# Four-layer MetaFormer on one core: units taken in pairs, skip additions moved to VectorE, matmuls added around the attention, and its softmax weights split between PSUM and GpSimd

## Chip, core and metric

The kernel runs on one core of one Trainium2 chip. The metric is device time in microseconds (us) of one launch: the median over repeated runs, lower is better. The rows below come from one profiled execution of the same program.

## What is computed

The reference is a stack of four layers on an image batch of 8 x 64 channels x 16 x 16. Each layer is a convolution-like block followed by a mixture of experts (MoE) over the tokens. The parts that the change touches:

```python
# layers 0 and 2, the MoE: two of eight experts per token, and the token itself is kept (skip)
out = tokens
for e in range(E):
    h = jax.nn.gelu(tokens @ w1[e] + b1[e], approximate=False)
    y = h @ w2[e] + b2[e]
    out = out + combine[:, e:e + 1] * y
# layer 1, the conv block: dilated 3x3 attention, one head pair for each dilation 1, 2, 4, 8
for i, dil in enumerate(DILATIONS):
    attn = jnp.einsum('bhcl,bhcpl->bhlp', qr, ku) * SCALE
    attn = jax.nn.softmax(attn, axis=-1)
    out = jnp.einsum('bhlp,bhcpl->bhlc', attn, vu)
    feats.append(...)
```

A MoE's input is the layer norm of the residual `t`, and its output is added to `t`. So the residual gets `t + ln(t) + experts` in layers 0 and 2.

## The kernel before

**Tiling.** The 2048 tokens lie as 16 tiles of 128 rows (partitions) by 64 channels in `res` (residual) and `xn` (normed). All data stays on the chip. Each engine (PE, DVE, ACT, POOL, SP) has its own instruction list, written out by hand in program order, with semaphores between them. An engine takes its list strictly in order.

**Layer norm and split.** `ln` writes `xn` on DVE. `split` then cuts it in two f16 halves: ACT writes the high half (L377), DVE subtracts it for the low half (`low`, L601, four instructions of 256 columns). PE transposes both (L1180), ACT and DVE copy them to `xs` (L389, L611), and the router's matmuls (L1190) follow.

**A MoE with skip (m = 0 and 2), "turned units".** 16 units (four token chunks of 512 x four expert pairs). For unit k: `first` makes h (L1232, L1233: f16, 512 columns each), ACT takes the gelu (L436), `spread` makes the routing weights over the expert rows (L1241: 16 rows x 512 columns, from `cT`), DVE multiplies (L779) into `gw`, and `turned_second` multiplies by w2 (L1287: f32, two halves of 64 output rows). At the first unit of a chunk, L1282 adds the biases `b2s`. After a chunk ACT copies the sum out (L398), PE turns it back (`turn_back`, L1297), and DVE adds it to the residual (`residual`, L771). The order on PE is `first(k+1)`, `spread(k)`, `turned_second(k-2)`. `spread(k)` needs DVE to be done with unit k-2, since two banks (4 and 5) alternate.

The value `base = res + xn` that L771 adds to is made by GpSimd in one instruction of 1024 columns (`with_skip`, L319), which starts once `xn` is written. In layer 0 GpSimd then also scales and splits the weights of later layers (L294, L305). After the last unit of MoE 0 GpSimd clears the borders ("pads") of the key and value buffer `kvx` (L345, two memsets of 3072 columns).

**The attention of layer 1.** Keys and values are shifted by PE (L1433) and copied by ACT (L508). DVE makes the logit products (L990, 768 columns) for three tap rows r and four dilations i. It reduces those of r = 1 and 2 itself (L997), and PE sums those of r = 0 (L1439, eight f32 matmuls whose moving columns are 8 elements apart). DVE takes the maxima (L1003) and subtracts them (L1009), ACT takes the exponentials (L513) into `le`, in SBUF. DVE multiplies weights by values (L1032, 24 instructions of 384 columns, two for each i and r). PE sums the products of i = 0, 1, 2 (L1444, nine groups of three f32 matmuls), DVE sums the weights (L1041, L1043) and, for i = 3, the products (L1046). `outputs_in` (L1019) divides PE's sums. `keep_warm` (L1196) is a run of matmuls whose result nobody reads.

Of the kernel before, what the change touches and what calls it, by code (L numbers as in the profile page):

```python
# [6 lines left out]
P = 128  # L7
NT = B * H * W // P
HALF = NT // 2
NPIX = H * W  # L10
DILS = (1, 2, 4, 8)
# [61 lines left out]
def metaformer(nc: bass.Bass, dram, codebook, out):  # L73
# [6 lines left out]
    with ctx:  # L80
# [23 lines left out]

        WH, WL = {}, {}
        for _, name in SPLIT + [("", "mix"), ("", "projs")]:
# [90 lines left out]
        cT = sb("cT", [32, NT * P], fp16)  # L197
        b2s = sb("b2s", [16, 2, 64], fp16)
# [4 lines left out]
        HIGH_LAG, LAG, PLAIN_LAG, TURNED_LAG = 2, 5, 3, 2  # L203
# [19 lines left out]
            "h_out act_out cb_out weighted out_added routed b2_both acc_copied acc_T base_ready unit_high unit_low_vec unit_low_pool second_out acc_in "  # L223
            "logit_product logit_summed value_product tap_row_summed kv1_out kv1_in shift_out shift_in att_sub att_exp mix_set mix_out pb_out pbias_in "
# [41 lines left out]
        logit_slots = [slots[4 + n % 4] for n in range(4)] + slots[0:4] + [slots[4 + n % 4] for n in range(4)]  # L266

# [19 lines left out]
        def _(pool):  # L287
# [23 lines left out]
            nc.gpsimd.memset(minus[:, :], -WSCALE / 2).then_inc(S["consts_set"], 1)  # L311
            scale_weights(["wqkv"])
# [3 lines left out]
            def with_skip(m):  # L316

                pool.wait_ge(S["src_ready"], chunks * (SPL.index(f"ln{2 * m + 1}") + 1))
                nc.gpsimd.tensor_tensor(base[:, :, :], res[:, :, :], xn[:, :, :], ALU.add).then_inc(S["base_ready"], 1)  # L319

# [18 lines left out]
            with_skip(0)  # L339
# [19 lines left out]
            with_skip(2)  # L359
# [10 lines left out]
        def _(act):  # L370
# [35 lines left out]
            def moe(m):  # L406
# [23 lines left out]
                if m in SPREAD:  # L430
                    for k in range(N):
# [7 lines left out]
                        if k >= 6 and (k - 6) % units[m] == 0:  # L439
                            copy_out(m, (k - 6) // units[m])  # L440
# [120 lines left out]
        def _(dve):  # L561
# [199 lines left out]
            def turned_units(m):  # L761
                U, N = units[m], chunks * units[m]

                def residual(c):
# [3 lines left out]
                    if c == 0:  # L768
                        dve.wait_ge(S["base_ready"], m // 2 + 1)
# [853 lines left out]
```

## Time and profile before

| what | value |
|---|---|
| median of 3 runs | 502.57 us (501.96 to 503.05) |
| the profiled execution | 502.17 us, its span 500.4 us |
| mean granted TensorE clock | 0.843 of full |
| DVE busy | 422.6 us, 84% of the span |
| PE busy (matmul) | 371.1 us, 74% |
| ACT busy | 210.6 us, 42% |
| POOL busy | 141.9 us, 28% |

The engine that ends a stage changes from stage to stage, so the shares alone decide little: each stage has to be read by itself. The profiled execution's time is 1.8 us more than its span, which is what lies around the span.

### The profile page before, as it was taken

To read this page: it belongs to the slowest core of one execution; us is meant where nothing else is said; L and a number is where in the kernel's file an instruction comes from. 1 tells how busy PE (TensorE), PEld (TensorE's weight loads), DVE (VectorE), ACT (ScalarE), POOL (GpSimd) and SP (SyncE) were. 2 spreads that over 40 slices of the span, in tenths; PEclk is the share of its full clock that TensorE was granted. 3 is DMA by queue.
4 is the path that set the end of the run, shared out by engine and by line. 5 is a ranking of instruction groups with operands and counts; after the bars stand their busy time and mean duration, and the time that the engine had idled before them with its cause. 6 is when DMAs were issued, how large, how long until landed. Compare 5 with 4: busy or idle time off the path is not lost.

```text
span 500.4 us, 9065 instructions
## 1 busy us (share of the span) xinstructions
PE 371.1 (74%) x3258; PEld 194.8 (39%) x3258; DVE 422.6 (84%) x1512; ACT 210.6 (42%) x398; POOL 141.9 (28%) x127
## 2 busy tenths in 40 slices
PE   2848669947797656799997993880369969448996
PEld 1434423314236523356664662260133323114554
DVE  4788987598979988879999999888885497897997
ACT  1642024412401121478885883330034434217994
POOL 1720040040000000078885884011020003711552
PEclk9978779977887858799998997777579987559999
DMA  8700000000000000000000000000000000100000
GB/s 351 298 1 0 1 1 2 0 2 0 0 0 1 0 1 1 0 2 4 1 3 1 2 3 2 0 1 1 0 2 0 1 0 9 27 9 2 12 14 22
DMA packets 2860, 9.73 MB, mean 19 GB/s; under 512 B 512, under 2 KB 1152, under 8 KB 2688
## 3 DMA queue, kind: packets, MB, share of 16 engines
q1 hardware_dynamic: 1296, 5.21, 2.6%
q10 hardware_dynamic: 1008, 3.42, 1.7%
q0 software_dynamic: 512, 0.53, 0.5%
q8 instruction: 26, 0.43, 0.3%
q14 instruction: 18, 0.15, 0.1%
HBM read 8.63 MB, written 0.52 MB: 18 GB/s over the span
## 4 chain that ended last, share of the span: by engine, by line
DVE 32%; PE 17%; issue 7%; ACT 1%; DVEq 0%; ACTq 0%
DVE res L805 13%; PE bank L1232 3%; PE bank L1261 2%; DVE hx L1131 2%; PE bank L1196 2%; PE bank L1233 2%; DVE bst L616 2%; DVE rs L1116 1%; DVE rs L1130 1%; PE bank L1522 1%; PE bank L1520 1%; PE bank L1287 1%; DVE xt L601 1%; DVE kvx_mem L815 1%; DVE xn L632 1%
## 5 line engine op out<-in xcount | busy, mean ns | idle before, releaser
L1196 PE MATMUL bank<-xs 128*128 128x512 f16 x242 | 76.8, 486 | 61.0 <-DVE bst L616 56.0
L326 POOL TENSOR_TENSOR kvx_mem<-kvx_mem 128x512 f16<-128x512 f32 x64 | 74.0, 1159 | 120.7 <-ACT kvx_mem L459 120.7
L805 DVE SCALAR_TENSOR_TENSOR res<-bank,rp,res 128x64 f32<-128x64 f32 x384 | 83.4, 291 | 2.2
L1196 PEld LDWEIGHTS bank<-xs 128*128 128x128 f16 x242 | 28.1, 120 | 105.4 <-DVE bst L616 57.6
L1261 PE MATMUL bank<-w_high,kvx_mem 128*128 128x64 f16 x768 | 58.4, 194 | 2.3 <-POOL kvx_mem L326 1.7
L1261 PE MATMUL bank<-w_low,kvx_mem 128*128 128x64 f16 x768 | 58.1, 194 | 0.0
L1261 PEld LDWEIGHTS bank<-w_high,kvx_mem 128*128 128x128 f16 x768 | 50.8, 98 | 13.8 <-POOL kvx_mem L326 2.0
L1232 PE MATMUL bank<-xs,w_high 128*128 128x512 f16 x128 | 51.5, 402 | 4.6 <-DVE kvx_mem L815 4.6
L377 ACT ACTIVATE xt<-xn 128x256 f16<-128x256 f32 x32 | 11.6, 417 | 101.4 <-DVE xn L634 101.4
L1261 PEld LDWEIGHTS bank<-w_low,kvx_mem 128*128 128x128 f16 x768 | 49.0, 98 | 7.1 <-issue 0.3
L1233 PE MATMUL bank<-xs,w_low 128*128 128x512 f16 x128 | 51.3, 400 | 0.0
L454 ACT ACTIVATE kvx_mem<-bank 128x512 f32<-128x512 f32 x64 | 38.1, 596 | 23.8 <-PE bank L1233 23.8
L815 DVE SCALAR_TENSOR_TENSOR kvx_mem<-kvx_mem,bank 128x512 f32<-128x512 f32 x64 | 44.7, 700 | 3.9 <-ACT kvx_mem L454 3.7
L459 ACT ACTIVATE kvx_mem<-kvx_mem 128x512 f16<-128x512 f32 x64 | 39.6, 622 | 0.0
L426 ACT ACTIVATE kvx_mem<-bank,pack_r 128x512 f32<-128x512 f32 x64 | 37.8, 714 | 0.0
L779 DVE TENSOR_TENSOR kvx_mem<-kvx_mem,bank 128x512 f32<-128x512 f32 x32 | 21.6, 687 | 18.0 <-PE bank L1241 15.7
L363 POOL DMA_INDIRECT kvx_mem<-in_codebook,ix x16 | 15.5, 967 | 56.8 <-DVE ix L1151 53.7
L436 ACT ACTIVATE kvx_mem<-bank,pack_r 128x512 f32<-128x512 f32 x32 | 21.2, 681 | 18.4 <-PE bank L1233 17.5
L336 POOL TENSOR_TENSOR kvx_mem<-kvx_mem 128x512 f16<-128x512 f32 x16 | 18.6, 1163 | 36.0 <-ACT kvx_mem L426 36.0
L1180 PE MATMUL bank<-pack_half,xt 128*128 128x128 f16 x144 | 13.3, 234 | 17.5 <-DVE xt L601 17.3
L1233 PE MATMUL bank<-xs,wu_low 128*128 128x512 f16 x64 | 25.0, 390 | 0.0
L1232 PE MATMUL bank<-xs,wu_high 128*128 128x512 f16 x64 | 25.0, 390 | 0.0
(310 smaller groups left out, 723.9 us busy)
## 6 DMA issues: line engine op xcount, KB each, us to landing
kvx_mem<-in_m SPq DMA_DIRECT2D x1, 2560.0 KB, 13.7
pack_l<-in_l ACTq DMA_DIRECT2D x1, 898.5 KB, 18.6
kvx_mem<-in_m SPq DMA_DIRECT2D x1, 768.0 KB, 18.5
pack_c<-in_c ACTq DMA_DIRECT2D x1, 648.0 KB, 5.7
pack_l<-in_l SPq DMA_DIRECT2D x1, 586.5 KB, 15.4
pack_x<-in_x SPq DMA_DIRECT2D x1, 512.0 KB, 5.5
pack_half<-in_half ACTq DMA_DIRECT2D x1, 512.0 KB, 7.7
pack_c<-in_c ACTq DMA_DIRECT2D x1, 512.0 KB, 14.0
```

Source lines behind the costliest of these rows:

```text
L326: nc.gpsimd.tensor_tensor(gl[:, n % DEPTH, :], gw[:, n % DEPTH, :], gh[:, n % DEPTH, :], ALU.subtract).then_inc(S["unit_low_pool"], 1)
L426: nc.scalar.activation(dst[:, n % DEPTH, :], bank[k % 4][:, :], ACT.Gelu, bias=K["b1_3"][:, k % units[m]:k % units[m] + 1], scale=1 / WSCA ...
L436: nc.scalar.activation(g[:, n % DEPTH, :], bank[k % 4][:, :], ACT.Gelu, bias=K[f"b1_{m}"][:, k % units[m]:k % units[m] + 1], scale=1 / WSC ...
L454: nc.scalar.activation(g[:, n % DEPTH, :], bank[k % 2][:, :], ACT.Silu, scale=1 / WSCALE)\
L459: nc.scalar.activation(gh[:, n % DEPTH, :], gw[:, n % DEPTH, :], ACT.Copy)\
L779: V.tensor_tensor(gw[:, n % DEPTH, :], g[:, n % DEPTH, :], bank[4 + k % 2][:, :], ALU.mult)\
L805: last = V.scalar_tensor_tensor(res[:, x, :], bank[4 + j % 4][:, 64 * t:64 * t + 64], rp[:, x, e:e + 1], res[:, x, :], ALU.mult, ALU.add)
L815: V.scalar_tensor_tensor(gw[:, (n0 + k) % DEPTH, :], g[:, (n0 + k) % DEPTH, :], CSCALE / WSCALE, bank[2 + k % 2][:, :], ALU.mult, ALU.mult ...
L1196: T.matmul(bank[unused][:, :], xs[:, 0:P], xs[:, 0:512], start=True, stop=True)
L1232: T.matmul(dst[:, :], WH[name][:, P * un:P * un + P], x, start=True, stop=False)
L1233: mm = T.matmul(dst[:, :], WL[name][:, P * un:P * un + P], x, start=False, stop=True)
L1261: mm = T.matmul(out_bank[:, 64 * t:64 * t + 64], part[:, n % DEPTH, P * t:P * t + P], w[f"w2_{m}"][:, 64 * un:64 * un + 64], start=(cfg["s ...
```

## The change

It has these parts.

1. **Paired units** (MoE 0 and 2). PE takes two units at a time: `first` of two, `spread` of two, then `turned_second` of the two before. `spread` and the bias matmuls now read 128 rows of `cT`, `sel0` and `b2s` instead of 16; the rows above 16 are cleared by GpSimd at the start.
2. **Skip additions on VectorE.** `with_skip` is gone from GpSimd. DVE adds `xn` into `res` in four instructions of 256 columns for each of the two MoEs, between the units. GpSimd's weight work of layer 0 now waits for `b2_ready`, which DVE signals at the end of the routing.
3. **Pads.** GpSimd clears only the columns that are read (eight memsets of 96 to 768 columns) and does so once the first k/v projection is done.
4. **Warm attention.** `keep_warm(8)` ahead of the shifts, `keep_warm(10)` ahead of the logit sum.
5. **Attention weights.** For dilations 0 to 2 ACT writes the exponentials to PSUM (banks 0 to 2), and PE's sums move to banks 4 to 6. For dilation 3 they stay in SBUF, and GpSimd makes the products (six instructions of 384 columns). DVE sums the weights by additions in place of the reduction, after i = 1, and sums dilation 3's products by four additions in place of L1046.

```diff
-            with_skip(0)
+            pool.wait_ge(S["b2_ready"], 1)
             scale_weights(["convw", "cbT"])
             weight_lows(["convw", "cbT"])
-            pool.wait_ge(S["second_out"], chunks * units[0])
-            for x in (0, PADX + NT):
-                nc.gpsimd.memset(kvx[:, :, x:x + PADX, :, :].rearrange("p r x a c -> p r (x a c)"), 0.0)\
-                    .then_inc(S["pads_set"], 1)
+            pool.wait_ge(S["kv1_out"], 1)
+            for i, d in enumerate(DILS):
+                for x in (PADX - d, PADX + NT):
+                    nc.gpsimd.memset(kvx[:, :, x:x + d, :, 16 * i:16 * i + 16], 0.0).then_inc(S["pads_set"], 1)
+            pool.wait_ge(S["pads_set"], 8)
+            pool.wait_ge(S["att_exp"], 4)
+            for r in range(3):
+                for h in range(2):
+                    value_product(nc.gpsimd, slots[6 + r], le[:, 3, 3 * r:3 * r + 3, :], r, 3, h)\
+                        .then_inc(S["value_product_pool"], 1)
...
-                nc.scalar.activation(le[:, :, 3 * r:3 * r + 3, :], lg[:, :, 3 * r:3 * r + 3, :], ACT.Exp, scale=8 ** -0.5)\
+                nc.scalar.activation(exps(r)[:, 0:3, :, :], lg[:, 0:3, 3 * r:3 * r + 3, :], ACT.Exp, scale=8 ** -0.5)\
                     .then_inc(S["att_exp"], 1)
+            nc.scalar.activation(le[:, 3, :, :], lg[:, 3, :, :], ACT.Exp, scale=8 ** -0.5).then_inc(S["att_exp"], 1)
...
+                def add_skip(c):
+                    t = slice(4 * c, 4 * c + 4)
+                    V.tensor_tensor(res[:, t, :], res[:, t, :], xn[:, t, :], ALU.add).then_inc(S["skip_added"], 1)
...
-                else:
-                    outputs_in(i - 1)
-            seq(V.tensor_reduce(stk[:, :, 48:64], pool_prod[:, :].rearrange("p (t x c) -> p x c t", t=9, c=16), AX,
-                                ALU.add))
+                if i == 2:
+                    outputs_in(0)
+                    outputs_in(1)
+            outputs_in(2)
+            dve.wait_ge(S["value_product_pool"], 6)
+            row3 = pool_prod[:, 0:768]
+            seq(V.tensor_tensor(row3, row3, pool_prod[:, 768:1536], ALU.add))
+            seq(V.tensor_tensor(row3, row3, pool_prod[:, 1536:2304], ALU.add))
+            seq(V.tensor_tensor(row3[:, 0:256], row3[:, 0:256], row3[:, 256:512], ALU.add))
+            seq(V.tensor_tensor(stk[:, :, 48:64], row3[:, 0:256].rearrange("p (x c) -> p x c", c=16),
+                                row3[:, 512:768].rearrange("p (x c) -> p x c", c=16), ALU.add))
...
-                    for k in range(N + TURNED_LAG):
-                        if early_units <= k + ahead < N:
-                            first(k + ahead)
-                        if k < N:
-                            spread(k)
-                        j = k - TURNED_LAG
-                        if j >= 0:
-                            turned_second(j)
-                            if j > U and j % U == 1:
-                                turn_back(j // U - 1)
+                    for k in range(0, N + 2, 2):
+                        if early_units <= k + 2 < N:
+                            first(k + 2)
+                            first(k + 3)
+                        if k < N:
+                            spread(k)
+                            spread(k + 1)
+                        if k >= 6 and k % U == 2:
+                            turn_back(k // U - 1)
+                        if k >= 2:
+                            turned_second(k - 2)
+                            turned_second(k - 1)
...
+            keep_warm(8, unused=5)
             pe.wait_ge(S["kv1_in"], 8)
...
+            keep_warm(10, unused=3)
             pe.wait_ge(S["logit_product"], 4)
```

**PE in MoE 0, two units in the middle (before).** L1232 and L1233 are `first`, L1241 is `spread`, L1287 is `turned_second`.

```order
L1232 MATMUL bank1<-xs,w1_0_high 128x512
L1233 MATMUL bank1<-xs,w1_0_low 128x512
L1241 MATMUL bank4<-cT,pack_half 128x512
L1287 MATMUL bank7<-kvx_mem,pack_w2 64x256 x2
L1232 MATMUL bank2<-xs,w1_0_high 128x512
L1233 MATMUL bank2<-xs,w1_0_low 128x512
L1241 MATMUL bank5<-cT,pack_half 128x512
L1287 MATMUL bank7<-kvx_mem,pack_w2 64x256 x2
```

**The same place in the changed kernel.** The lines are now L1273 and L1274 (`first`), L1282 (`spread`) and L1328 (`turned_second`).

```order
L1273 MATMUL bank0<-xs,w1_0_high 128x512
L1274 MATMUL bank0<-xs,w1_0_low 128x512
L1273 MATMUL bank1<-xs,w1_0_high 128x512
L1274 MATMUL bank1<-xs,w1_0_low 128x512
L1282 MATMUL bank4<-cT,pack_half 128x512
L1282 MATMUL bank5<-cT,pack_half 128x512
L1328 MATMUL bank6<-kvx_mem,pack_w2 64x256 x4
```

Two units' matmuls of one kind now stand together, so the kind changes three times for two units and not six times.

**DVE in the attention (before),** from the value products of dilation 0 to the sum for dilation 3 (`ls` holds the sums of weights, `q` is the output buffer):

```order
L1032 TENSOR_TENSOR big<-lg_mem,kvx_mem 128x48x8 x6
L1041 TENSOR_REDUCE ls<-lg_mem 128x128
L1043 RECIPROCAL ls<-ls 128x128
L1032 TENSOR_TENSOR big<-lg_mem,kvx_mem 128x48x8 x6
L1019 TENSOR_TENSOR q<-bank,ls 128x16x16
L1032 TENSOR_TENSOR big<-lg_mem,kvx_mem 128x48x8 x6
L1019 TENSOR_TENSOR q<-bank,ls 128x16x16
L1032 TENSOR_TENSOR pool_prod<-lg_mem,kvx_mem 128x48x8 x6
L1019 TENSOR_TENSOR q<-bank,ls 128x16x16
L1046 TENSOR_REDUCE q<-pool_prod 128x16x16
```

**The same place in the changed kernel** (L277 is `value_product`):

```order
L277 TENSOR_TENSOR big<-bank,kvx_mem 128x48x8 x12
L1070 TENSOR_TENSOR tops_mem<-lg_mem 128x96
L1071 COPY tops_mem<-bank 128x288
L1072 TENSOR_TENSOR tops_mem<-tops_mem,lg_mem 128x96
L1073 TENSOR_TENSOR tops_mem<-bank,tops_mem 128x288
L1074 TENSOR_TENSOR tops_mem<-bank,tops_mem 128x288
L1075 TENSOR_TENSOR ls<-tops_mem 128x128
L1076 TENSOR_TENSOR ls<-ls,tops_mem 128x128
L1077 RECIPROCAL ls<-ls 128x128
L277 TENSOR_TENSOR big<-bank,kvx_mem 128x48x8 x6
```

Six products are gone from DVE, and the weight sums stand behind dilation 1 instead of dilation 0.

**GpSimd's list (before),** from layer 0's weight work to MoE 1:

```order
L319 TENSOR_TENSOR base<-res,xn 128x1024
L294 TENSOR_SCALAR pack_l<-pack_l 128x576
L294 TENSOR_SCALAR pack_l<-pack_l 128x256
L305 TENSOR_TENSOR convw_low<-pack_l,convw_high 128x512
L305 TENSOR_TENSOR convw_low<-pack_l,convw_high 128x64
L305 TENSOR_TENSOR cbT_low<-pack_l,cbT_high 128x256
L345 MEMSET kvx_mem 128x3x1024 x2
```

**The same stretch in the changed kernel:**

```order
L308 TENSOR_SCALAR pack_l<-pack_l 128x576
L308 TENSOR_SCALAR pack_l<-pack_l 128x256
L319 TENSOR_TENSOR convw_low<-pack_l,convw_high 128x512
L319 TENSOR_TENSOR convw_low<-pack_l,convw_high 128x64
L319 TENSOR_TENSOR cbT_low<-pack_l,cbT_high 128x256
L357 MEMSET kvx_mem 128x3x2x16 x2
L357 MEMSET kvx_mem 128x3x4x16 x2
L357 MEMSET kvx_mem 128x3x8x16 x2
L357 MEMSET kvx_mem 128x3x16x16 x2
L277 TENSOR_TENSOR pool_prod<-lg_mem,kvx_mem 128x48x8 x6
```

The addition of 1024 columns is gone, the memsets are smaller, and six products are new.

## Rows read from the trace of the kernel before

**Rows 1.** The page, part 1: busy time of each engine, share of span, instructions.
```profile
PE 371.1 (74%) x3258; PEld 194.8 (39%) x3258; DVE 422.6 (84%) x1512; ACT 210.6 (42%) x398; POOL 141.9 (28%) x127
```

**Rows 2.** Timeline at three splits: start us, us, engine, line, operation, names, count.
```profile
65.04 2.34 POOL L319 TENSOR_TENSOR base<-res,xn 128x1024 f32<-128x1024 f32 x1 [36.72 <-DVE xn L634]
65.05 5.24 DVE L601 TENSOR_TENSOR xt<-xn,xt 128x256 f16<-128x256 f32 x4
...
201.15 1.43 DVE L601 TENSOR_TENSOR xt<-xn,xt 128x256 f16<-128x256 f32 x4
...
365.75 3.58 DVE L601 TENSOR_TENSOR xt<-xn,xt 128x256 f16<-128x256 f32 x4
365.79 2.58 POOL L319 TENSOR_TENSOR base<-res,xn 128x1024 f32<-128x1024 f32 x1 [23.67 <-DVE xn L634]
```

**Rows 3.** Timeline behind the last units of MoE 0, then of MoE 2.
```profile
105.31 5.26 POOL L345 MEMSET kvx_mem<- 128x3072 f32 x2 [34.23 <-PE bank L1287]
...
105.54 5.05 DVE L592 TENSOR_SCALAR step_part<-rstd 128x8 f32<-128x8 f32 x1
...
405.13 0.16 DVE L592 TENSOR_SCALAR step_part<-rstd 128x8 f32<-128x8 f32 x1
```

**Rows 4.** Timeline of PE over one unit of MoE 0.
```profile
85.41 0.39 PE L1232 MATMUL bank<-xs,w_high 128*128 128x512 f16 x1
...
85.64 0.38 PE L1233 MATMUL bank<-xs,w_low 128*128 128x512 f16 x1
...
85.95 0.38 PE L1241 MATMUL bank<-cT,pack_half 16*128 16x512 f16 x1
...
86.26 0.65 PE L1287 MATMUL bank<-kvx_mem,pack_w 128*64 128x256 f32 x4
...
86.85 0.39 PE L1232 MATMUL bank<-xs,w_high 128*128 128x512 f16 x1
```

**Rows 5.** The chain that ended last, MoE 2: start us, us, what.
```profile
385.92 0.58 PE bank L1287 x4
...
398.62 0.58 PE bank L1287 x4
```

**Rows 6.** Waits of DVE: us in total, times, longest.
```profile
DVE kvx_mem L779 <- PE bank L1241: 15.7, 20, 1.1
```

**Rows 7.** Timeline of the attention's value part.
```profile
152.49 2.89 DVE L1032 TENSOR_TENSOR big<-lg_mem,kvx_mem 128x384 f32<-128x384 f32 x6
...
153.56 14.48 PE L1444 MATMUL bank<-big,pack_c 128*128 128x256 f32 x54 [3.76 <-DVE big L1032]
155.29 2.11 DVE L1041 TENSOR_REDUCE ls<-lg_mem 128x128 f32<-128x1152 f32 x1
...
168.14 0.42 DVE L1019 TENSOR_TENSOR q<-bank,ls 128x256 f32<-128x256 f32 x1 [0.54 <-PE bank L1444]
168.49 4.03 DVE L1046 TENSOR_REDUCE q<-pool_prod 128x256 f32<-128x2304 f32 x1
```

**Rows 8.** Timeline of the attention's logit part.
```profile
138.41 11.39 PE L1439 MATMUL bank<-big,pack_c 128*128 128x384 f32 x16 [2.53 <-DVE big L990]
...
140.25 0.96 DVE L990 TENSOR_TENSOR big<-q,kvx_mem 128x768 f32<-128x768 f32 x1
```

**Rows 9.** Windows of 1 us: PE, PEld, DVE, ACT, POOL busy, granted clock.
```profile
141.00:142.00 1.00, 1.00 (x2) 0.31 (x1) 0.96 (x2) 0.00 (x0) 0.00 (x0) 0.65 0.00 0
...
158.00:159.00 1.00, 1.00 (x4) 0.85 (x3) 0.96 (x3) 0.00 (x0) 0.00 (x0) 0.62 0.00 0
```

**Rows 10.** Costliest groups: busy us, mean ns of one, idle before.
```profile
L326 POOL TENSOR_TENSOR kvx_mem<-kvx_mem 128x512 f16<-128x512 f32 x64 | 74.0, 1159 | 120.7 <-ACT kvx_mem L459 120.7
...
L815 DVE SCALAR_TENSOR_TENSOR kvx_mem<-kvx_mem,bank 128x512 f32<-128x512 f32 x64 | 44.7, 700 | 3.9 <-ACT kvx_mem L454 3.7
```

**Rows 11.** Timeline at the end of MoE 2's routing.
```profile
377.00 0.36 DVE L739 SCALAR_TENSOR_TENSOR c<-rp,c 128x64 f16<-128x64 f32 x2
...
378.70 1.06 PE L1318 MATMUL bank<-pack_half,c 128*16 128x128 f16 x16
```

More of the change, by code:

```diff
@@ L103, in metaformer @@
             K[name] = packs["half"][0:rows, at:at + cols]
+        at, _, cols = where["sel0"]
+        K["sel0_rows"] = packs["half"][0:P, at:at + cols]
         WH, WL = {}, {}
@@ L266, in metaformer, with exps, value_product @@
         logit_slots = [slots[4 + n % 4] for n in range(4)] + slots[0:4] + [slots[4 + n % 4] for n in range(4)]
+        def exps(r):
+            return bank[r][:, 0:384].rearrange("p (i s g) -> p i s g", i=4, s=3)
+        def value_product(engine, product, weights, r, i, h):
+            return engine.tensor_tensor(
+                product.rearrange("p (s x h c) -> p s x h c", s=3, h=2, c=8)[:, :, :, h, :],
+                weights.rearrange("p s (x h) -> p s x h", h=2)[:, :, :, h].unsqueeze(3).broadcast_to([P, 3, NT, 8]),
+                taps(r, i, 1, 16 * i + 8 * h, 16 * i + 8 * h + 8), ALU.mult)
         def taps(r, i, a, c0, c1):
@@ L438, in moe @@
                                              scale=1 / WSCALE).then_inc(S["act_out"], 1)
[L439 to L440 removed]
+                        if k >= 7 and k % units[m] == 3:
+                            copy_out(m, k // units[m] - 1)
                     copy_out(m, chunks - 1)
@@ L780, in turned_units @@
                         .then_inc(S["weighted"], 1)
-                    if m == 0 and 3 <= k < 7:
-                        constants[k - 3]()
-                    if k in (8, 12):
-                        residual(k // 4 - 2)
+                    if k == 1:
+                        add_skip(0)
+                    if k == 3:
+                        add_skip(1)
+                    if k == 5:
+                        add_skip(2)
+                    if k == 7:
+                        residual(0)
+                        add_skip(3)
+                    if m == 0 and k == 4:
+                        mix_weights()
+                    if m == 0 and k == 6:
+                        projection_weights()
+                    if m == 0 and k == 8:
+                        last_bias()
+                    if m == 0 and k == 9:
+                        phi_sums()
+                    if k == 11:
+                        residual(1)
                     if k == 13:
@@ L1019, in outputs_in @@
                 V.tensor_tensor(s3[:, i, :, :, :],
-                                bank[2 + i][:, 0:256].rearrange("p (x h c) -> p x h c", h=2, c=8),
+                                bank[4 + i][:, 0:256].rearrange("p (x h c) -> p x h c", h=2, c=8),
                                 bc(total[:, i, :, :], 8), ALU.mult)
-            for i in range(4):
+            for i in range(3):
                 for r in range(3):
@@ L1448, in _ @@
                 if name == "stk":
-                    keep_warm(8, unused=5)
+                    keep_warm(8, unused=3)
                 else:
```

62 lines of the change are left out of this document (30 added, 32 removed).

## The prediction, made blind

> **What bounds the kernel now.** I read the busy shares first. DVE works 84% of the span and PE 74% [rows 1], so no engine is full, and the gain of an edit has to be read where it stands. I then read the timeline at the places that the change touches, and looked in each for an instruction that takes longer than its shape does elsewhere.
>
> At the split of layer 0, four L601 take 5.24 us beside GpSimd's L319. The same four take 1.43 us in layer 1, where GpSimd has nothing to do, and 3.58 us in layer 2, again beside L319 [rows 2]. Behind MoE 0 a DVE instruction on eight columns takes 5.05 us beside GpSimd's two memsets of 5.26 us. Behind MoE 2, without memsets, it takes 0.16 us [rows 3]. So DVE is held by GpSimd at three places, all on the path that sets the end.
>
> In the MoEs with skip PE sets the pace. One unit takes 1.44 us from L1232 to the next L1232 [rows 4], eight units take 12.70 us with the bias and turn-back matmuls in them [rows 5], and DVE waits 15.7 us in 20 waits for `spread` [rows 6].
>
> In the attention's value part PE sets the end too. DVE comes to the last L1019 and waits 0.54 us for PE's sums, and then reduces for 4.03 us alone [rows 7].
>
> **The change part by part.**
>
> *Skip additions.* Without L319 four L601 should take 1.43 us at both splits: 5.24 - 1.43 = 3.8 us in layer 0 and 3.58 - 1.43 = 2.15 us in layer 2 [rows 2]. In layer 0 the weight work behind L319 held the later L601 too (5.24 is more than 2.34 + 1.43), and it moves behind `b2_ready`, where DVE reads banks. The new additions are eight of 256 columns, 0.42 us each as L1019 of that size [rows 7], 3.4 us of DVE in all. They are hidden: per pair of units DVE has 2 x 0.69 us of products against 2.88 us of PE. If that cover were gone they would cost 3.4 us. In MoE 0 units 6 and 7 now carry a residual, an addition and the projection weights between them, which is more than a pair's time. I charge 0.3 us.
>
> The Trainium skill (SBUF — State Buffer, "Who interferes with whom") says that DVE and GpSimd share a port pair as an exclusive lock: a DVE instruction with two SBUF inputs waits for a GpSimd instruction that reads SBUF, for its whole length. The two splits agree with it: the excess in layer 2 is 2.15 us beside an L319 of 2.58 us. By the rule the sum would be the same here.
>
> *Pads.* The memsets leave the path: 5.05 - 0.16 = 4.9 us [rows 3]. The eight new ones clear 2 x (96 + 192 + 384 + 768) = 2880 columns. By 5.26 us for 6144 columns [rows 3] that is 2.5 us. They start at the first k/v projection and have over 4 us until DVE's first logit product, so they are hidden. If not, they cost what is left over, at most about 1 us.
>
> *Paired units.* The starts in [rows 4] give the steps: L1232 to L1233 0.23 us, L1233 to L1241 0.31, L1241 to L1287 0.31, L1287 to L1232 0.59. A step between two like matmuls of 512 columns is 0.23, one to another kind 0.31. A pair needs four `first` and two `spread` matmuls: five steps of 0.22 to 0.23 between them and one of 0.31 out, and two seconds of 0.55 to 0.59: 5 x 0.225 + 0.31 + 1.15 = 2.59 us, 0.29 less than 2.88. The step from `first` to `spread` is taken as 0.23 since `spread` now fills all 128 rows. Three pairs and a half lie in steady state until unit 13, after which DVE computes statistics: 1.0 us. Unit 13's product now follows unit 12's after 0.69 us and not after 1.44: 0.75 us. The bias matmuls lose one change of shape each: 0.2 us. Together 2.0 us per MoE, 4.0 for both. The bounds: nothing but the 0.75 us (0.8 per MoE), if the steps stay as they are; and 3.2 per MoE, if the seconds' 0.59 falls to 0.44 back to back.
>
> The Trainium skill (TensorEngine Tiling (Array Packing), "Key Properties") says that a change of tiling mode drains TensorE. The 0.08 us between the steps agrees with it, and it would give what the row gives.
>
> *Warm attention.* It should bring nothing by itself. PE's logit sum takes 16 records in 11.39 us [rows 8], an even 0.7 us each, although the granted clock rose from half to full in the middle of it, near 141.7 us [rows 9]. So its pace does not hang on the clock. It starts when DVE's fourth product is there, at 138.4 us, and the ten matmuls ahead of it fit into the 2.53 us that PE idled [rows 8], if warm. The shifts are not waited for. I take zero; were the ten cold (0.43 us each) they would cost up to 1.8 us.
>
> *Attention weights.* DVE starts the products at 152.5 us and needs 2.89 us per dilation [rows 7]. Products of dilations 0 and 1 end at 158.3. GpSimd starts about 153.5, when the fourth exponential is there. A product of 384 columns on it costs 0.88 us by L319's 2.34 us for 1024 columns, 0.97 by 2.58 us [rows 2], 0.87 by L326 [rows 10]. I take 0.93, since rows at these shapes span so little: six end at 159.1. DVE's own products now read one input from a bank. L815, which does so too, takes 700 ns for 512 columns with GpSimd at work [rows 10], so they should not be held. The first addition of weights reads SBUF twice and should wait 0.8 us for GpSimd. The sums are then 2 x 0.25 + 3 x 0.45 + 2 x 0.29 = 2.4 us (each 0.15 us plus 1.05 ns a column, from 0.42 us for 256 and 0.96 us for 768 [rows 7, 8]) where L1041 took 2.11, and the reciprocal stays. Dilation 2's products end at 165.5. PE starts at 153.6, cold until about 158.6 [rows 9], and its 54 records need until 168.0 as before [rows 7], since it is fed late by no more than the slack it has (0.2 us). So L1019 for dilation 2 still starts at 168.1: the six products and the idle time taken off DVE bring nothing. What is left is the end: 4.03 us become 2 x 0.96 + 2 x 0.42 = 2.8 us, so 1.2 us are saved. The bounds: -1.2 us (a loss) if GpSimd's products are 1.3 us each and the sums wait for all of them, and +2.4 us if PE is warm from the start.
>
> *The clock at MoE 2.* DVE had the routing weights ready at 377.4 us, and PE came to them at 378.7, since its `keep_warm` ran at half clock [rows 11]. With the shorter idle time at the split it may stay warm. Between 0 and 1.3 us, I take 0.6.
>
> **The sum:** 3.8 + 2.15 + 4.9 + 4.0 - 0.3 + 1.2 + 0.6 = 16.3 us. The profiled execution took 502.2 us, so it becomes 485.9. The median of the runs is 0.4 us above that execution, so 486.3.
>
> **The rivals.**
>
> *A, DVE becomes the pace of the paired units.* Two waits per pair fall together: PE waits for both products before it goes on, and DVE has additions between them. For it: 15.7 us of waits look like slack only if they lie at the right places. Against it: 1.4 us of products per pair against 2.6 of PE. Then the pairs bring nothing: 486.3 + 4.0 = 490.3 us. Chance 0.15.
>
> *B, GpSimd's products are slower and hold the sums.* Their operands are broken into runs of eight with a broadcast, and no row shows that on GpSimd. At 1.5 us each GpSimd ends at 162.5, the sums start 3.4 us later than I take them, and PE, starved, ends 2.2 us late: 488.5 us. Chance 0.15.
>
> *C, slower than before.* The same mechanism, at 5 us a product. GpSimd would end at 153.5 + 6 x 5 = 183.5, DVE's sum for dilation 3 starts then and not at 168.5, and with the weight sums held piece by piece and PE fed later the stage ends some 17 us late: 504 us. That takes five times the price of any row, and it decides from about 4.9 us a product. Chance 0.02.
>
> *D, the holds are not GpSimd's, or they return.* The moved weight work (3.8 us) or the new memsets hold other DVE instructions as long as the old ones did. For it: GpSimd does the same weight work. Against it: at both places DVE reads banks. Half of 10.9 us would come back: 491.8 us. Chance 0.05.
>
> *E, the pairs bring their upper bound and the value sums run warm:* 486.3 - 2.4 - 1.2 = 482.7 us. Chance 0.13.
>
> **How the numbers follow.** My forecast has 0.5, with a range of its own of 484.3 to 488.3. The predicted time is 486.3. The range that should hold 8 in 10 goes from 482.5 (E) to 490.4 (A) and leaves out C, D and a little on both sides. A measurement of this kernel tells about 0.2% (1 us) from no change. Only C ends above that: slower 0.02. Within 0.2%: 0.01. Faster: 0.97.
>
> **What the changed profile would show.** Four L601 (now L617) at 1.4 us at the splits of layers 0 and 2; no long DVE instruction behind MoE 0; a pair of units in 2.6 us; the logit sum still in 11.4 us at full clock, which would prove its pace is not the clock's; GpSimd's six products ending near 159 us minus what was saved before, and DVE still waiting for PE ahead of the last `outputs_in`. It would be wrong if DVE's products slow down beside GpSimd, or if PE's steps inside a pair do not shrink.

## The result, and the profile after

The changed kernel took 484.94 us (median of 4 runs, 482.13 to 485.97) beside 502.81 us for the kernel before: a ratio of 0.963, 95% interval 0.959 to 0.968. Measured again (`after_again`), it took 485.45 us beside 502.96, 0.966 (0.964 to 0.967). The prediction was 486.3 us, its range 482.5 to 490.4. The profiled execution took 485.97 us, its span 484.2. A few executions of a kernel take over 1.5% more than its fastest one, at a lower mean granted clock (two of the four of `skip_alone`, the profiled one among them, and one of the six of `single_units`), and the ratios leave them out.

The page of the changed kernel, its part on busy time (answers to [rows 1]):

```profile
PE 362.4 (75%) x3276; PEld 199.3 (41%) x3276; DVE 410.1 (85%) x1523; ACT 209.0 (43%) x399; POOL 140.7 (29%) x139
```

DVE (VectorE) and PE (TensorE) together got some 21 us lighter, and the shares hardly moved. What counts is where the time lay. The timeline of the changed kernel at the places of [rows 2] and [rows 3]: the split of layer 0, the eight-column instruction behind MoE 0, GpSimd's pads, and the split of layer 2.

```profile
66.77 1.43 DVE L617 TENSOR_TENSOR xt<-xn,xt 128x256 f16<-128x256 f32 x4
...
99.41 0.16 DVE L608 TENSOR_SCALAR step_part<-rstd 128x8 f32<-128x8 f32 x1
...
111.33 2.77 POOL L357 MEMSET kvx_mem<- 128x96 f32 x8 [31.41 <-PE bank L1232]
...
354.65 1.43 DVE L617 TENSOR_TENSOR xt<-xn,xt 128x256 f16<-128x256 f32 x4
```

Both splits take 1.43 us (5.24 and 3.58 in [rows 2]). The pads are cleared from 111.33 us, and DVE's first logit product comes at 115.81. The instruction that took 5.05 us takes 0.16.

PE in MoE 0, one pair of units (answers to [rows 4]):

```profile
82.01 0.39 PE L1273 MATMUL bank<-xs,w_high 128*128 128x512 f16 x1
82.24 0.38 PE L1274 MATMUL bank<-xs,w_low 128*128 128x512 f16 x1
82.45 0.38 PE L1273 MATMUL bank<-xs,w_high 128*128 128x512 f16 x1
82.67 0.38 PE L1274 MATMUL bank<-xs,w_low 128*128 128x512 f16 x1
82.88 0.59 PE L1282 MATMUL bank<-cT,pack_half 128*128 128x512 f16 x2
83.41 1.08 PE L1328 MATMUL bank<-kvx_mem,pack_w 128*64 128x256 f32 x8
84.42 0.39 PE L1273 MATMUL bank<-xs,w_high 128*128 128x512 f16 x1
```

Read the starts: from one pair's first L1273 to the next one's is 84.42 - 82.01 = 2.41 us, where two units took 2.88. PE has no gap in these rows, so it still sets the pace. The waits of DVE (answers to [rows 6]: us in total, times, longest) are no longer for PE's `spread` but for ACT's gelu, which waits for PE's `first`:

```profile
DVE kvx_mem L799 <- ACT kvx_mem L451: 7.3, 7, 1.2
...
DVE q L1052 <- PE bank L1490: 2.7, 1, 2.7
DVE tops_mem L1036 <- PE bank L1485: 2.6, 1, 2.6
```

The attention's value part (answers to [rows 7]): GpSimd's six products, PE's sums, DVE's last scaling of PE's sums, and the four additions that took the place of L1046.

```profile
142.48 5.04 POOL L277 TENSOR_TENSOR pool_prod<-lg_mem,kvx_mem 128x384 f32<-128x384 f32 x6 [28.38 <-ACT lg_mem L530]
142.51 14.56 PE L1490 MATMUL bank<-big,pack_c 128*128 128x256 f32 x54 [3.75 <-DVE big L277]
...
157.10 0.42 DVE L1052 TENSOR_TENSOR q<-bank,ls 128x256 f32<-128x256 f32 x1 [2.73 <-PE bank L1490]
157.44 0.95 DVE L1084 TENSOR_TENSOR pool_prod<-pool_prod 128x768 f32<-128x768 f32 x1
158.43 0.96 DVE L1085 TENSOR_TENSOR pool_prod<-pool_prod 128x768 f32<-128x768 f32 x1
159.42 0.43 DVE L1086 TENSOR_TENSOR pool_prod<-pool_prod 128x256 f32<-128x256 f32 x1
159.88 0.43 DVE L1087 TENSOR_TENSOR q<-pool_prod 128x256 f32<-128x256 f32 x1
```

The work freed on DVE turned into a wait of 2.73 us for PE, and the additions stand behind that wait.

**The same span by stages.** I cut each trace at DVE instructions that all kernels have, and give the time from the start of one to the start of the next, in us. The first six stages hold what the change touches; in the last four before and after run the same code. Columns to the right are experiments told below.

| stage | before | after | skip_alone | pads_alone | pairs16_alone | rows16 | single_units |
|---|---|---|---|---|---|---|---|
| MoE 0: split to `cT` copy | 15.16 | 10.69 | 10.69 | 15.43 | 15.48 | 10.71 | 10.68 |
| MoE 0: first product to first statistics | 19.17 | 15.91 | 31.05 | 19.18 | 17.29 | 17.14 | 19.18 |
| MoE 0: first to second statistics | 12.92 | 8.01 | 9.46 | 8.01 | 12.91 | 8.01 | 8.01 |
| attention: first value product to last scaling | 20.06 | 18.90 | 19.57 | 19.57 | 19.57 | 18.60 | 19.06 |
| MoE 2: split to `cT` copy | 14.05 | 10.43 | 10.61 | 12.63 | 14.05 | 10.42 | 11.81 |
| MoE 2: first product to last residual | 26.75 | 23.47 | 26.74 | 26.74 | 24.70 | 24.71 | 26.73 |
| start to the norm ahead of MoE 0 | 62.27 | 63.98 | 63.29 | 63.66 | 63.62 | 64.73 | 64.01 |
| last scaling to the statistics ahead of MoE 1 | 20.74 | 21.50 | 20.51 | 20.45 | 20.23 | 21.49 | 21.28 |
| MoE 1 and convolution, to the statistics ahead of MoE 2 | 164.60 | 164.96 | 163.61 | 163.71 | 164.38 | 164.77 | 164.48 |
| MoE 2's last residual to the first use of the quantiser's output | 25.11 | 27.11 | 25.09 | 26.37 | 26.00 | 25.79 | 25.12 |

Before to after, the six touched stages gained 4.47 + 3.26 + 4.91 + 1.16 + 3.62 + 3.28 = 20.7 us. The four untouched ones lost 1.71 + 0.76 + 0.36 + 2.00 = 4.8 us. The rest (short stages, not in the table) gave 0.3, which makes the 16.2 us between the spans. So the forecast's 16.3 us came out right by two things that cancel: the touched stages gave 4.4 us more, and the stages outside took that back.

What took it back is PE's granted clock. The windows over the start of the quantiser's matmuls, first before, then after (the stretch and its length in us, PE busy and number of matmuls, granted clock; the last two columns are of the DMA):

```profile
417.00:419.00 2.00, 1.88 (x12) 1.00 0.00 0
...
421.00:423.00 2.00, 2.00 (x11) 0.65 0.08 16
423.00:425.00 2.00, 2.00 (x9) 0.50 0.10 25
```
```profile
399.00:401.00 2.00, 1.99 (x12) 0.87 0.00 0
401.00:403.00 2.00, 2.00 (x9) 0.50 0.00 0
```

They begin at 417.1 us before and at 399.0 after. In both the clock falls to half (1.2 of 2.4 GHz) in the middle of busy work: 4.5 us in before, less than 2 us in after, and VectorE waits for what comes of it. All of the 2.0 us of that stage arise there, since the matmuls begin 8.8 us after the last residual in both. The stage from the start to the norm shows the same without any change in the work near it: it took between 62.3 and 64.7 us over all 14 traces of this study, and the kernels that have the old code there and beyond it (skip_alone, pads_alone, pairs16_alone) lie at 63.3 to 63.7 too.

The stage behind the attention (from the last scaling to the statistics ahead of MoE 1) is another matter. Its code is the same everywhere, but its time goes with the value part ahead of it: five traces with the old value code have 20.23 to 20.74 us there, mean 20.45, and seven with the new one and its additions behind the wait have 21.04 to 21.85, of which six (without `warm_values`, told below) have a mean of 21.44. The last 3.8 us of the stage in the changed kernel, then in `values_on_vector`, which has the old value part:

```profile
178.00:181.80 3.80, 1.87 (x32) 0.58 0.02 4
```
```profile
176.00:179.80 3.80, 1.55 (x39) 1.00 0.02 4
```

With the new value part the clock is at half again under the matmuls that close the stage.

### The profile page after: what moved, and what is told of

It is laid out like the page before. It is cut to its first block, busy times and chain, and to the rows that moved or that the text cites. A ratio compares the mean times of both kernels' runs of the same rounds, so it can differ in the third digit from the quotient of the medians.

```text
span 484.2 us, 9134 instructions
## 1 busy us (share of the span) xinstructions
PE 362.4 (75%) x3276; PEld 199.3 (41%) x3276; DVE 410.1 (85%) x1523; ACT 209.0 (43%) x399; POOL 140.7 (29%) x139
## 4 chain that ended last, share of the span: by engine, by line
DVE 31%; PE 18%; issue 7%; ACT 1%; DVEq 0%; ACTq 0%
DVE res L840 10%; PE bank L1302 4%; PE bank L1273 4%; PE bank L1274 4%; DVE hx L1172 2%; DVE bst L632 2%; PE bank L1568 2%; PE bank L1566 2%; DVE rs L1157 2%; DVE rs L1171 1%; DVE xn L648 1%; PE bank L1328 1%; DVE xn L650 1%; DVE kvx_mem L850 1%; DVE xt L617 1%
## 5 line engine op out<-in xcount | busy, mean ns | idle before, releaser
L840 DVE SCALAR_TENSOR_TENSOR res<-bank,rp,res 128x64 f32<-128x64 f32 x384 | 81.8, 274 | 2.2
L1273 PE MATMUL bank<-xs,w_high 128*128 128x512 f16 x128 | 49.4, 386 | 6.0 <-DVE kvx_mem L850 5.9
L1274 PE MATMUL bank<-xs,w_low 128*128 128x512 f16 x128 | 49.4, 386 | 0.0
L850 DVE SCALAR_TENSOR_TENSOR kvx_mem<-kvx_mem,bank 128x512 f32<-128x512 f32 x64 | 43.1, 675 | 4.1 <-ACT kvx_mem L469 3.9
L441 ACT ACTIVATE kvx_mem<-bank,pack_r 128x512 f32<-128x512 f32 x64 | 37.8, 710 | 0.0
L1273 PE MATMUL bank<-xs,wu_high 128*128 128x512 f16 x64 | 24.9, 389 | 0.0
L1274 PE MATMUL bank<-xs,wu_low 128*128 128x512 f16 x64 | 24.8, 387 | 0.0
L451 ACT ACTIVATE kvx_mem<-bank,pack_r 128x512 f32<-128x512 f32 x32 | 19.7, 675 | 9.3 <-PE bank L1274 8.7
```

The source lines that it names most:

```text
L441: nc.scalar.activation(dst[:, n % DEPTH, :], bank[k % 4][:, :], ACT.Gelu, bias=K["b1_3"][:, k % units[m]:k % units[m] + 1], scale=1 / WSCA ...
L451: nc.scalar.activation(g[:, n % DEPTH, :], bank[k % 4][:, :], ACT.Gelu, bias=K[f"b1_{m}"][:, k % units[m]:k % units[m] + 1], scale=1 / WSC ...
L840: last = V.scalar_tensor_tensor(res[:, x, :], bank[4 + j % 4][:, 64 * t:64 * t + 64], rp[:, x, e:e + 1], res[:, x, :], ALU.mult, ALU.add)
L850: V.scalar_tensor_tensor(gw[:, (n0 + k) % DEPTH, :], g[:, (n0 + k) % DEPTH, :], CSCALE / WSCALE, bank[2 + k % 2][:, :], ALU.mult, ALU.mult ...
L1273: T.matmul(dst[:, :], WH[name][:, P * un:P * un + P], x, start=True, stop=False)
L1274: mm = T.matmul(dst[:, :], WL[name][:, P * un:P * un + P], x, start=False, stop=True)
```

## The experiments

Twelve kernels ran in three groups; those of one group share the runs of the kernel before. First one part of the change alone, or one undone.

**skip_alone: the skip additions alone, on the kernel before.**

```diff
-            with_skip(0)
+            pool.wait_ge(S["b2_ready"], 1)
...
-            with_skip(2)
...
+                    if k in (1, 2, 7, 9):
+                        add_skip((1, 2, 7, 9).index(k))
```

> The kernel before with one part of the change: VectorE makes the skip additions inside the MoE loop and GpSimd starts its weight work only after the routing. The forecast's terms: 3.8 us in layer 0 and 2.15 in layer 2, and some 0.3 given back to the four additions where they do not fit a wait: 5.7 us off, a time of about 497.1. By the view that the holds return elsewhere (rival D), 0 to 3. In the trace the four splits at about 65 and 365 us should take 1.43 us together in each place, and the time from there to the end of the routing should fall by 3.8 to 4.1 us in layer 0.

Measured: 503.53 us (496.17, 503.42, 503.64 and 509.04) beside 503.27, ratio 0.989 (0.976 to 1.003): by the runs nothing gained, where 497.1 was expected. In the trace both splits take 1.43 us, as forecast, and the stages at the splits fell by 4.47 and 3.44 us, more than the forecast 3.8 to 4.1 and 2.15. But MoE 0's units took 31.05 us instead of 19.17. The windows of this kernel over MoE 0, then of the kernel before:

```profile
80.00:85.00 5.00, 5.00 (x21) 0.67 0.00 0
85.00:95.00 10.00, 10.00 (x32) 0.50 0.00 0
...
105.00:115.00 10.00, 10.00 (x32) 0.50 0.00 0
```
```profile
85.00:95.00 10.00, 10.00 (x54) 1.00 0.00 0
```

PE was busy all the time and yet at half clock: 32 matmuls in 10 us where the kernel before has 54. So this loss is the clock's and not the additions': VectorE waits up to 2.43 us for `spread` there. The one execution of 496.17 us had a mean granted clock of 0.855, the other three 0.828 to 0.830; it is 7.1 us faster than the kernel before (503.27), but has no trace. What the part is worth is thus seen in the trace's stages at the splits; the runs do not show it.

The same trace gives a second reading, since the old memsets now meet other VectorE instructions. They ran from 117.24 to 122.50 us:

```profile
117.93 0.76 DVE L595 TENSOR_TENSOR xt<-xn,xt 128x256 f16<-128x256 f32 x2
...
119.06 1.11 DVE L610 BATCH_NORM_STATS2 bst<-res 128x6 f32<-128x64 f32 x8
...
120.58 1.94 DVE L619 TENSOR_SCALAR mean<-mean 128x8 f32<-128x8 f32 x1
```

A subtraction with two SBUF inputs (L595) and the statistics ran at their usual pace beside the memset; the first `TENSOR_SCALAR` stood until the memset ended (120.58 + 1.94 = 122.52). The Trainium skill (SBUF — State Buffer, "Who interferes with whom") makes just this distinction: a VectorE instruction with two SBUF inputs contends with a GpSimd instruction that reads SBUF and not with one that only writes it, while `tensor_scalar` can enter a two-port mode, which contends with GpSimd. The trace agrees on both, though it does not show the mode.

**pads_alone: the pads alone, on the kernel before** (the memsets of the diff, nothing else).

> The kernel before with one part: the pads are set in eight small memsets after the first attention projection. The forecast: 4.9 us off, about 497.9, and the 8-column VectorE instruction of the first half's root takes 0.16 us instead of 5.05. If that stall was not GpSimd's, or moves to another VectorE instruction beside the new memsets, 0 to 2 us off.

Measured: 497.58 us (497.2 to 498.86) beside 503.27, ratio 0.986 (0.977 to 0.994). The stage between the two statistics fell by 4.91 us, and the instruction took 0.16 us. The forecast's 4.9 holds. MoE 2's split to `cT` also fell, by 1.42 us, although the pads are nowhere near and the four L601 still take 3.57 us there. That is the clock again: granted 0.86 over this stage, 0.76 in the kernel before, 1.00 in the changed kernel.

**pairs16_alone: the paired order alone, 16 rows kept.**

> The kernel before with the paired order of PE alone; the spread stays on 16 rows, and the residual and copy positions are those of the change. By the forecast (2.59 us a pair, regrouping is what pays) 4.0 us off, about 498.8, with MoE 2's pairs at 2.6 us. The changed kernel's trace has 2.42 us a pair: if the 128 rows give the other 0.17 us, this run shows 2.6 a pair; if regrouping gives it all, 2.42 and 6.5 us off, about 496.3. If VectorE had set the pace all along, nothing.

Measured: 497.71 us (494.9, 495.07, 500.35 and 500.66), ratio 0.983 (0.974 to 0.993). The two higher ones had a mean granted clock of 0.836 and 0.839, the two lower ones 0.858. By stages the units gained 1.88 us in MoE 0 and 2.05 in MoE 2, so 3.9 us for pairing, and 2.6 are missing to the changed kernel's 6.5.

**rows16: the changed kernel, `spread` and bias on 16 rows again.**

```diff
-  T.matmul(bank[4 + k % 2][:, :], K["sel0_rows"][:, P * un:P * un + P], cT[:, 512 * c:512 * c + 512],
+  T.matmul(bank[4 + k % 2][:, :], sel[:, P * un:P * un + P], cT[0:2 * E, 512 * c:512 * c + 512],
```

> The changed kernel with the spread and the bias matmuls on 16 rows again, pairs kept. Each MoE's units took 3.26 us less in the changed kernel than before, and 1.9 to 2.05 less with pairs alone: if the 128 rows give the other 1.25, this kernel takes 1.25 us longer in each of two MoEs (15.91 to 17.2 us and 23.47 to 24.7), 487.4. If what is missing from the pairs alone was the place of the skip additions or of the small weight work, the two stretches stay at 15.9 and 23.5.

Measured: 487.56 us (485.88 to 487.58) beside 485.45 for `after_again`. The two unit stages took 17.14 and 24.71 us, 1.23 and 1.24 us more. The missing part is found. Its PE timeline shows where:

```profile
83.01 0.39 PE L1273 MATMUL bank<-xs,w_high 128*128 128x512 f16 x1
...
83.67 0.38 PE L1274 MATMUL bank<-xs,w_low 128*128 128x512 f16 x1
83.98 0.60 PE L1282 MATMUL bank<-cT,pack_half 16*128 16x512 f16 x2
84.51 1.08 PE L1328 MATMUL bank<-kvx_mem,pack_w 128*64 128x256 f32 x8
85.53 0.39 PE L1273 MATMUL bank<-xs,w_high 128*128 128x512 f16 x1
```

From the last `first` to `spread` it is 0.31 us with 16 rows and 0.21 with 128 (82.67 to 82.88 above); a pair takes 2.52 us (83.01 to 85.53) against 2.41. A pair with the bias and turn-back matmuls in it takes 3.22 us (from 85.53) against 2.83 (from 84.42 in the changed kernel). Three plain pairs and two of these make 1.1 of the 1.23 us.

**single_units: the changed kernel, units one by one on 16 rows.**

> The changed kernel with the units one by one on 16 rows, as before, skip additions still on VectorE. By the sum of the parts the two stretches grow by 3.3 us each, to 19.2 and 26.7: 491.5. The kernel with the skip additions alone ran the whole of MoE 0 at granted clock 0.5 in its trace and lost 11.9 us there. If single units without the wait for GpSimd at the split bring that about, most runs here are at 500 or above with the first stretch near 31 us; if it was chance of that one kernel, they are near 491.5.

Measured: 492.23 us (489.35 to 493.06, and one execution of 518.66) beside 485.45 for `after_again`. Both unit stages are back at 19.18 and 26.73 us: pairs and rows together are 3.27 us per MoE, of which 2.0 are the pairs' and 1.24 the rows'. MoE 0 was not at half clock in this trace. So the MoE at half clock of `skip_alone` is not what single units bring whenever GpSimd's wait at the split is gone. It befell the profiled execution of that kernel, by their mean clock two more, and perhaps the one of 518.66 us here (mean clock 0.797), which has no trace.

**values_on_vector: the changed kernel with the old value part.**

> The changed kernel with the value part of the kernel before: exponentials in SBUF, all 24 products on VectorE, one reduction of 4.03 us for the fourth dilation; GpSimd makes no products. By the forecast the part is worth 1.2 us: this kernel is 1.2 us slower than the changed one, about 486.1, and the stretch from the first product to the last group's scaling goes back from 18.9 to 20.1 us. If GpSimd's products cost VectorE more elsewhere than the trace shows, it is as fast or faster.

Measured: 484.19 us (481.45 to 484.76), ratio 0.957 (0.948 to 0.965): no slower than the changed kernel as far as runs can tell, where 1.2 us more was expected. In the trace the stage took 19.58 us. Five traces with the old value code have 20.06 and four times 19.57 or 19.58, mean 19.67; six with the new one have 18.60 to 19.28, mean 18.93. That is 0.7 us. But the stage right behind it takes 1.0 us more in the same traces (21.44 against 20.45, see above): together 40.4 us with the new value part and 40.1 with the old. So in these traces the part brings nothing, which agrees with the runs.

The spread within each kind is the clock's too. The lines show the stretch from 4.5 to 6.5 us after the first product. In `before` and in the changed kernel (first and second) the clock was still at half, and the last scaling of PE's sums came 15.66 us after that product in both. In `pads_alone` (last) it was full, and there it came after 15.17:

```profile
157.00:159.00 2.00, 2.00 (x6) 0.56 0.00 0
```
```profile
146.00:148.00 2.00, 2.00 (x6) 0.53 0.00 0
```
```profile
154.00:156.00 2.00, 2.00 (x10) 0.97 0.00 0
```

**no_warm: the changed kernel without the two added `keep_warm`.**

> The changed kernel without its two added runs of dummy matmuls in attention (8 before the shifts, 10 before the sums of the logits). Forecast: they are worth nothing, since the sum of the logits takes 11.39 us at either clock: about 484.9. By the view that they do warm attention: the logit sum gets longer or ends later, and 1 to 3 us are lost (486 to 488).

Measured: 483.62 us (482.82 to 485.94), ratio 0.959 (0.954 to 0.964). The logit stage took 25.62 us (25.63 with them) and the value stage 18.76 (18.60 to 19.28 in the traces with them). They bring nothing, as forecast.

The next kernels try what the profile after suggests.

**row3_early: the four additions ahead of the wait.**

```diff
-            outputs_in(2)
             dve.wait_ge(S["value_product_pool"], 6)
...
+            outputs_in(2)
```

> The changed kernel with the four additions that sum GpSimd's products put ahead of the scaling of the third dilation, into the 2.73 us in which VectorE waits for PE's last sums. If PE sets the end there, as the forecast has it, the additions (2.65 us by the trace) leave the path and 2.6 us are saved: about 482.3. If VectorE's wait is only moved on, 0.

Measured: 479.19 us (478.46 to 480.06), ratio 0.949 (0.944 to 0.954). VectorE in this kernel:

```profile
152.87 0.75 DVE L1052 TENSOR_TENSOR q<-bank,ls 128x256 f32<-128x256 f32 x2
153.53 0.95 DVE L1083 TENSOR_TENSOR pool_prod<-pool_prod 128x768 f32<-128x768 f32 x1
...
156.43 0.42 DVE L1052 TENSOR_TENSOR q<-bank,ls 128x256 f32<-128x256 f32 x1
```

No wait is left before the second L1052, and the value stage took 16.07 us, 2.83 less than in the changed kernel's trace. The median fell by 5.7, more than the 2.6 expected: in this trace the stage behind the attention took 20.2 us instead of 21.5 and the one of the quantiser 24.9 instead of 27.1, both with the same code.

**warm_values: 14 dummy matmuls between the logit sum and the value sums.**

```diff
             mm.then_inc(S["logit_summed"], 1)
+            keep_warm(14, unused=3)
```

> The changed kernel with 14 dummy matmuls between the sum of the logits and the sums of the values. If the value sums are late because their first 5.6 us run at granted clock 0.5, they end about 2.6 us earlier and VectorE's 2.73 us wait there falls to about 0: 482.3. If the clock falls nevertheless, or the dummies hold up the first sum, no gain, up to 1 us lost.

Measured: 482.46 us (480.62 to 482.93), ratio 0.955 (0.950 to 0.960). The stage took 17.89 us: 1.0 gained, not 2.6. PE's rows show why:

```profile
141.27 8.04 PE L1491 MATMUL bank<-big,pack_c 128*128 128x256 f32 x36 [0.73 <-DVE big L277]
...
150.67 4.15 PE L1491 MATMUL bank<-big,pack_c 128*128 128x256 f32 x18 [1.36 <-DVE big L277]
```

The clock held, and 36 records of the sums took 8.04 us. Then PE waited 1.36 us for the third dilation's products, which stand behind the sums of weights and the reciprocal on VectorE. With PE at full clock the bound moved to VectorE's order.

**logit_contiguous: the products that PE sums written in contiguous runs.**

```diff
-            products = big[:, 0:3072].rearrange("p (i g c) -> p i g c", i=4, c=8)
...
-                mm = T.matmul(bank[0][:, 0:384], ident, products[:, :, :, c], start=(c == 0), stop=(c == 7))
+                mm = T.matmul(bank[0][:, 0:384], ident, big[:, 384 * c:384 * c + 384], start=(c == 0), stop=(c == 7))
```

VectorE writes them with a step of 384 columns, in eight instructions of 384 columns.

> The changed kernel with the four products that PE sums written as eight contiguous runs of 384 columns (eight instructions of 384 columns in place of four of 768), so that PE reads columns side by side instead of every eighth. If the step through the columns makes a matmul take 0.69 us a record at either clock, the sum falls from 11.39 to some 5 us and VectorE's wait of 2.60 us goes: 482.3, less if scattered writes make the products slower. If the sum is bound by the count of columns, 11.4 us stays and nothing changes.

Measured: 485.33 us (483.89 to 487.03), ratio 0.961 (0.956 to 0.966). The timeline of this kernel, the products and PE's sum:

```profile
123.06 5.47 DVE L1027 TENSOR_TENSOR big<-q,kvx_mem 128x384 f32<-128x384 f32 x8
...
128.59 7.12 PE L1490 MATMUL bank<-big,pack_c 128*128 128x384 f32 x16 [3.98 <-DVE big L1027]
```

PE's sum fell from 11.39 to 7.12 us and VectorE's wait of 2.60 us is gone, but the products went from 3.6 us to 5.47. The stage gained 0.8 us (24.78 against 25.5 to 25.6), too little to see in the runs.

**contiguous_row3 and after_again: both edits together, and the changed kernel beside them.**

> The changed kernel with the two edits that gained: the fourth dilation's additions ahead of the wait for PE's last sums (2.83 us off that part in its trace) and the logit products written as contiguous runs (0.85 us off). They are in different stretches and should add up: 3.7 us less than the changed kernel run beside it, about 481.2. If the first alone had its 5.7 us lower median from clock luck, that shows here as 3.7; if not, 6 to 7.

> The changed kernel once more, to have its time beside the three that follow and to see how much of a trace's stages moves with nothing changed: 484.9 us, between 482 and 486. The stages whose code is the same in all kernels should differ from the first trace only by PE's granted clock: the norm ahead of MoE 0 between 62.3 and 64.0 us, the stretch from MoE 2's end to the quantiser's end between 24.9 and 27.4.

Measured: contiguous_row3 477.27 us (476.72 to 477.9), ratio to the kernel before 0.949 (0.948 to 0.951); after_again 485.45 (484.71 to 486.54). It is 8.2 us faster than the changed kernel, where 3.7 was expected. The touched stages gave 0.77 and 2.88 us, 3.65 together, as expected. The other 4.8 us between the two traces (spans of 475.2 and 483.6 us) lies in stages that share their code: 1.6 behind the attention, 1.3 in the quantiser, 1.1 in MoE 1 and the convolution, 0.85 before MoE 0. All five of its executions are within 1.2 us of each other. So the clock's share is not only scatter from run to run; it goes with the kernel, presumably with the moments at which its dense stretches begin. That was not tested by itself.

## Why the prediction was right, point by point

**The splits** (3.8 and 2.15 us): right. The split instructions fell to 1.43 us in both places, in the changed kernel and with the part alone. (The stages around them fell by more, see the clock at MoE 2 below.)

**The pads** (4.9 us): right, 4.91 us in the stage, with the part alone as well. The new memsets (2.77 us, forecast 2.5) are hidden.

**Paired units** (2.0 us per MoE): the mechanism was right and the term too small. It measured 3.27 us per MoE, just above the bound of 3.2. Two parts of the working were off. A pair took 2.41 us and not 2.59, for the most part because the eight back-to-back `turned_second` records take 1.01 us and not 1.15: the step of 0.59 out of a unit [rows 4] held a change of shape that no longer exists inside the pair. And I credited the 128 rows with one step of 0.08 us a pair and with 0.2 for the bias; they brought 1.24 us per MoE (`rows16`). Pairing alone, on 16 rows, gave 1.9 to 2.05.

**Units 6 and 7** (0.3 us lost): wrong, no loss is seen. MoE 0 with the small weight work and MoE 2 without it gained the same, 3.26 and 3.28 us.

**Attention weights** (1.2 us): the end was right, the sum too large. From the last scaling of PE's sums to the last group's it went from 4.4 us (168.14 to 172.55) to 3.24. DVE waited for PE as forecast, and GpSimd's products took 0.84 us each (forecast 0.93). (The prediction has PE at half clock until 158.6 us; [rows 9] give 158.8.) At a like clock, `before` against the changed kernel, the stage gained 1.16 us, as forecast; over several traces it gained 0.7. What the forecast left out is the stage behind it, at nothing without a reason: there the new value part costs 1.0 us in the same traces, at half clock, so that the part brings nothing in total. Its upper bound (2.4 us with PE warm from the start) was wrong too: `warm_values` kept the clock full and gained 1.0 us, since VectorE's order then set the end.

**Warm attention** (nothing): right, by `no_warm`. The logit sum took 11.39 us again, with the clock at half at its start and full after it.

**The clock at MoE 2** (0.6 us, 0 to 1.3): it measured 1.4, just above the bound: from the end of the routing to the `cT` copy it went from 2.80 to 1.38 us. PE starts on the routing weights at once:

```profile
363.70 0.36 DVE L755 SCALAR_TENSOR_TENSOR c<-rp,c 128x64 f16<-128x64 f32 x2
363.98 1.06 PE L1359 MATMUL bank<-pack_half,c 128*16 128x128 f16 x16 [1.33 <-DVE c L755]
```

The reason that I gave, the shorter idle time at the split, does not decide it: `pads_alone` has the long split and gained 1.42 us there, and `single_units` has the short one and lacks 1.4 of the gain. Of eleven traces with the short split nine have the gain, of three with the long one one has it, so the split may still shift the odds; that stays open. For a single kernel it is luck of the clock, and belongs with the next point.

**What the prediction lacked** is the clock in the stages that nothing touches. It took 4.8 us of the profiled execution (0.8 of them behind the attention, and those go with the new value part), and the forecast had no term for it. That the total fell within 1.4 us of the forecast is owed to this loss as much as to the working: of the rivals, the paired units' half of E came true (A, VectorE as their pace, did not: PE has no gap), and with these stages as before the time would have been near 481 by my estimate (485.9 - 4.8), below the range. That the forecast came out is in part luck. B and C fell with GpSimd's 0.84 us a product, D with the table's stages.

## What to carry to other kernels

Before looking for a better engine split, look for an instruction that takes several times what its shape takes elsewhere in the same trace: three such places gave 11 us here, and the size of the instructions' excess could be read to 0.1 us before the edit. When an edit takes work off an engine, look at what that engine then waits for, and move independent work into the wait: four additions moved by one line gave 2.8 us, where the whole rewriting of the attention weights gave nothing. Judge edits of one or two us by the same stage in several traces, together with the stage right behind it, and not by medians, since here the clock in untouched stages moved the total by up to 5 us.

## What the runs showed of the hardware

**With a step in the moving operand TensorE gained nothing from its full clock.** With every eighth f32 column, 16 records of 384 columns took 11.39 us, an even 0.69 us from start to start after the first step, and the pace did not follow the clock (changed kernel, windows over the sum, columns as above; records that reach over a border count in both):

```profile
127.00:131.00 4.00, 3.63 (x6) 0.57 0.00 0
131.00:139.00 8.00, 7.76 (x12) 1.00 0.00 0
```

With contiguous columns the pace is twice as fast at full clock as at half. PE's weight loads in contiguous_row3, one per record, and its windows:

```profile
131.08 0.34 PEld L1490 LDWEIGHTS bank<-big,pack_c 128*128 128x128 f32 x1 [0.30 <-issue]
131.72 0.34 PEld L1490 LDWEIGHTS bank<-big,pack_c 128*128 128x128 f32 x1 [0.30 <-issue]
...
133.64 1.86 PEld L1490 LDWEIGHTS bank<-big,pack_c 128*128 128x128 f32 x6 [0.30 <-issue]
```
```profile
131.00:133.00 2.00, 2.00 (x5) 0.50 0.00 0
...
134.00:136.00 2.00, 2.00 (x7) 1.00 0.00 0
```

Starts are 0.64 us apart at first, and six follow in 1.86 us (some 0.32 us apart) later. The stepped operand takes 0.69 either way: little is lost at half clock, over half the speed at full. The Trainium skill (SBUF — State Buffer, "Specifications (TRN2)") says that full bandwidth needs two hits or more in each 16-byte line; a step of 32 bytes has one, and the runs agree that it costs.

**The clock can stay at half through 30 us of busy PE** (`skip_alone`, above). What brings it about stays open. None of the 47 executions of the changed kernel and of its variants with paired units was slower than 488 us, while the single-unit kernel had one of 518.66 in six, and the kernel before some of 506 to 509 in two of the three groups. That is suggestive and no more.

**A GpSimd memset does not stop every VectorE instruction.** Beside it, a subtraction with two SBUF inputs ran at its usual pace and a `TENSOR_SCALAR` of eight columns stood until its end, for 5.05 us in [rows 3] and 1.94 in `skip_alone`.
